# Layernorm statistics copied across the partitions by DMA instead of by TensorE, and other orders of work in front of the output projection

## What is computed

```
x = x + attention(layernorm(x), ctx, mask, Wq, Wk, Wv, Wo)   # 32 query heads, 8 key/value heads of 128, rope,
                                                             # logits = 30 * tanh(logits * 0.0884 / 30), mask, softmax
x = x + ffn(layernorm(x), W_base, b_base, W_router, A, B)    # one linear layer with a top-2 of 8 low-rank experts
layernorm(x) = (x - mean(x)) / sqrt(var(x) + 1e-5)           # mean and variance of each token (row) over 1024 features
```

## Time and profile before

| | us |
|---|---|
| median of 3 executions | 2128.66 (2127.95 to 2129.84) |
| the profiled execution, its own time | 2128.13 |
| its span in the trace | 2126.3 |
| TensorE busy in the span | 2118.6 |
| VectorE busy | 1652.2 |
| ScalarE busy | 879.3 |
| GpSimd busy | 338.8 |
| DMA | 508.52 MB, mean 239 GB/s |

### The profile page before, as it was taken

How to read it: one execution, slowest core, us unless ns; L and a number is a source line. 1 busy time by engine, 2 the same in 40 slices (tenths; PEclk the granted TensorE clock), 3 DMA queues, 4 the chain that set the end, 5 groups by cost and what they waited for, 6 DMA issues and landing times.

```text
span 2126.3 us, 26531 instructions
## 1 busy us (share of the span) xinstructions
PE 2118.6 (100%) x9429; PEld 1721.3 (81%) x9429; DVE 1652.2 (78%) x2387; ACT 879.3 (41%) x1353; POOL 338.8 (16%) x438
## 2 busy tenths in 40 slices
PE   9999999999999999999999999999999999999999
PEld 8888888888888888877777877777787777888887
DVE  6969759999986666677877888998999898856533
ACT  3323343222241111157555556655666566423211
POOL 0000025666350000003111111111111110100000
PEclk9999999999999999999999999999999999999999
DMA  8778667777685566679656666678557854596761
GB/s 314 244 247 287 237 208 303 277 282 267 258 320 210 211 216 212 219 249 314 226 190 197 232 238 198 198 257 290 199 171 264 295 197 153 191 359 247 283 248 61
DMA packets 198820, 508.52 MB, mean 239 GB/s; under 512 B 20896, under 2 KB 46624, under 8 KB 196640
## 3 DMA queue, kind: packets, MB, share of 16 engines
q1 hardware_dynamic: 172448, 424.43, 56.6%
q0 software_dynamic: 26240, 82.38, 11.6%
HBM read 357.26 MB, written 149.16 MB: 238 GB/s over the span
## 4 chain that ended last, share of the span: by engine, by line
PE 97%; DMA 1%; ACT 1%; DVE 0%; issue 0%; SPq 0%; ACTq 0%; DVEq 0%
PE pq L235 32%; PE pq L236 31%; PE pq L237 31%; PE pq L1300 1%; PE pq L1959 0%; PE pq L1958 0%; DMA raw<-gran 0%; DMA raw<-ctxT 0%; DMA RB<-rD 0%; DMA rD<-r 0%; PE pq L411 0%; ACT Rh L1225 0%; SPq L1122 0%; DVE Rl L1230 0%; ACT Pf L1439 0%
## 5 line engine op out<-in xcount | busy, mean ns | idle before, releaser
L235 PE MATMUL pq<-Ah,Rh 128*128 128x512 f32 x1024 | 399.0, 390 | 0.0
L237 PE MATMUL pq<-Ah,Rl 128*128 128x512 f32 x1024 | 398.5, 389 | 0.0
L236 PE MATMUL pq<-Al,Rh 128*128 128x512 f32 x1024 | 398.5, 389 | 0.0
L235 PE MATMUL pq<-Xq,qW 128*128 128x512 f32 x896 | 348.7, 389 | 0.5 <-issue 0.4
L236 PE MATMUL pq<-Xq,qW 128*128 128x512 f32 x896 | 348.6, 389 | 0.0
L237 PE MATMUL pq<-Xq,qW 128*128 128x512 f32 x896 | 348.5, 389 | 0.0
L1230 DVE TENSOR_TENSOR Rl<-raw,Rh 128x1024 fp32r<-128x1024 f32 x176 | 214.2, 1218 | 91.4 <-ACT Rh L1225 91.0
L1225 ACT ACTIVATE Rh<-raw 128x1024 fp32r<-128x1024 f32 x176 | 185.3, 1054 | 166.2 <-PE pq L237 128.2
L235 PEld LDWEIGHTS pq<-Ah,Rh 128*128 128x128 f32 x1024 | 192.2, 188 | 41.9 <-ACT Y L1451 0.8
L237 PEld LDWEIGHTS pq<-Ah,Rl 128*128 128x128 f32 x1024 | 192.2, 188 | 40.5
L236 PEld LDWEIGHTS pq<-Al,Rh 128*128 128x128 f32 x1024 | 192.2, 188 | 40.1
(11 more groups left out here) (243 smaller groups left out, 3935.2 us busy)
## 6 DMA issues: line engine op xcount, KB each, us to landing
raw<-gran SPq DMA_DIRECT2D x177, 512.0 KB, 4.4
QSD<-qW SPq DMA_DIRECT2D x64, 512.0 KB, 2.9
qD<-qt SPq DMA_DIRECT2D x128, 256.0 KB, 5.4
qW<-QSD SPq DMA_DIRECT2D x64, 512.0 KB, 3.4
qf<-qD SPq DMA_DIRECT2D x64, 512.0 KB, 6.1
RB<-rD POOLq DMA_DIRECT2D x128, 256.0 KB, 4.2
qraw<-gran SPq DMA_DIRECT2D x48, 512.0 KB, 5.2
kD<-kst SPq DMA_DIRECT2D x32, 512.0 KB, 5.7
```

The costliest lines, as they stand in the source:

```text
L235: e.matmul(dst, lh, rh, start=first, stop=False, skip_group_check=more)
L236: e.matmul(dst, lh, rl, start=False, stop=False, skip_group_check=more)
L237: return e.matmul(dst, ll, rh, start=False, stop=last, skip_group_check=more)
```

## The change

The statistics are spread by DMA. A new function `rows_spread` on POOL's queue, once for each chunk, writes each of the two columns of `mv` (mean and reciprocal deviation) to `rD` in DRAM, element by element, and reads it back as a row on all partitions, straight into `xl0` or `xl1`. The mean comes without the minus sign, so the addition on DVE and POOL becomes a subtraction. The diagonals on DVE, their splits on ACT and DVE, the 16 matmuls with ones and the 8 copies from PSUM are gone.

In front of O: on ACT the high part of query block 5 stands ahead of granule 9, and granule 11 behind the tanh of score block 4; on DVE the low part of block 5 stands ahead of granule 9's, those of granules 10 and 11 come earlier, and value product 0 leaves PSUM after product 1 and behind the low part of P. On POOL the stores of values 0 and 1 stand behind the loads of `RB`. On SP the loads of granules 12, 13 and 14 are put at steps -7 to -5 and that of group 1's values at -5.

```diff
-        DIAG = {15: 0, 16: 1, 38: 2, 39: 3}
-        SPREAD = {18: (0, 0), 19: (0, 1), 20: (1, 0), 21: (1, 1), 41: (2, 0), 42: (2, 1), 43: (3, 0), 44: (3, 1)}
...
-                if n in SPREAD:
-                    c, i = SPREAD[n]
-                    whole, high, low = diagonal(c, i)
-                    t.wait_ge("kv_dgl", (c, i))
...
-                    e.matmul(ps[7][:, :], ones[:, :], high[:, :], start=True, stop=False)
-                    e.matmul(ps[7][:, :], ones[:, :], low[:, :], start=False, stop=True).then_inc(*t.tick("kv_sp", (c, i)))
...
-                        t.wait_ge("kv_x", (i, 0))
-                        e.tensor_tensor(y, y, m[:, :], ALU.add).then_inc(*t.tick("kv_xa", (0, k, i, kk // 4)))
+                        t.wait_ge(f"d_xl{i}0", i)
+                        e.tensor_tensor(y, y, m[:, :], ALU.subtract).then_inc(*t.tick("kv_xa", (0, k, i, kk // 4)))
...
+        def rows_spread(t, c):
+
+            e = t.e
+            t.wait_ge("kv_rs", (c, 5))
+            for i in range(2):
+                e.dma_start(rD[i, c, :].rearrange("(b p) -> p b", p=P), mv[:, c, :, i], allow_slow_non_contiguous=True).then_inc(
+                    *t.tick(f"d_mv{i}", c, 16))
+            if c > 1:
+                t.wait_ge("kv_xn", (0, 3, c % 2))
+            for i in range(2):
+                t.wait_ge(f"d_mv{i}", c)
+                e.dma_start((xl1 if c % 2 else xl0)[i][:, :], bc(rD[i, c:c + 1, :], [P, T])).then_inc(*t.tick(f"d_xl{c % 2}{i}", c, 16))
+
         def pool_kv(t):
             e = t.e
+            rows_spread(t, 0)
+            rows_spread(t, 1)
             for k, i in XBLOCK.values():
...
+            rows_spread(t, 2)
+            rows_spread(t, 3)
...
-            if at == -10:
-                w_high(t, 11)
             if at == -9:
                 v_high(t, at)
...
+            if at == -10:
+                w_high(t, 11)
...
                 if at == -11:
+                    q_high2(t, 5)
                     w_high(t, 9)
-                    q_high2(t, 5)
...
-        V_EVAC = {-9: (0, 1), -8: (2,), -7: (3,), -6: (4,), -4: (5,), -2: (6,), 0: (7,)}
+        V_EVAC = {-9: (1, 0), -8: (2,), -7: (3,), -6: (4,), -4: (5,), -2: (6,), 0: (7,)}
...
+            if at == -9:
+                w_low(t, 11)
             for gi, b in S_AT.get(at - 1, []):
...
             if at == -9:
-                w_low(t, 11)
                 row_sums(t, 0)
-                v_low(t, at)
+                v_low(t, at, (1,))
...
             if at == -11:
                 q_low2(t, 4)
+                q_low2(t, 5)
                 w_low(t, 9)
-                q_low2(t, 5)
...
+            if at == -9:
+                v_low(t, at, (0,))
...
-            v_store(t, at)
+            if at == -8:
+                v_store(t, -9)
+            if at != -9:
+                v_store(t, at)
...
-            if at == -9:
+            if at == -5:
                 load_v(t, 1)
...
-            WL_AT.setdefault(at + 1, []).append(x)
+            WL_AT.setdefault({12: -7, 13: -6, 14: -5}.get(x, at + 1), []).append(x)
```

More of the change, by code:

```diff
@@ L40 @@
     "low": ("kv_lo", "q_lo", "w_lo"), "high": ("kv_hi", "q_hi", "w_hi"), "rope": ("kv_rope", "q_rope"),
-    "prep": ("kv_dg", "kv_dgl", "kv_bn", "kv_rs", "kv_mask", "kv_xb", "set", "q_xl0", "q_xl2"), "kv_low": ("kv_kl", "kv_vl", "v_vl"),
-    "kv_high": ("kv_kh", "kv_vh", "v_vh"), "prep_act": ("kv_sq", "kv_dgh", "kv_x"), "p": ("a_exp", "a_ph"),
+    "prep": ("kv_bn", "kv_rs", "kv_mask", "kv_xb", "set", "q_xl0", "q_xl2"), "kv_low": ("kv_kl", "kv_vl", "v_vl"),
+    "kv_high": ("kv_kh", "kv_vh", "v_vh"), "prep_act": ("kv_sq",), "p": ("a_exp", "a_ph"),
     "top": ("f_lg", "f_m8", "f_ix", "f_pr", "f_ixf", "f_oh", "f_w", "f_wx", "f_r2"), "f_act": ("f_e", "f_h", "f_hwh"),
@@ L58 @@
 SHARED_DMA += [(f"d_rb{i}", [f"d_bx{i}"]) for i in range(4)]
+SHARED_DMA += [(f"d_{x}{i}", [f"d_{y}{i}"]) for x, y in (("rt", "mv"), ("rs", "xl0"), ("x2", "xl1")) for i in range(2)]
 SHARED_DMA += [(f"d_x1{k}", [f"d_xt{k}"]) for k in range(4)]
@@ L462, in act_kv @@
             for n in range(-1, NK + 3):
[L463 to L469, removed]
                 for p in range(NPC):
@@ L487, in act_kv @@
                         e.activation(rs4[:, 1 + c % 2], rs4[:, 0] if c % 2 == 0 else rs4[:, 3], ACT.Sqrt).then_inc(*t.tick("kv_sq", c))
[L488 to L493, removed]
                 if 0 <= n - 1 < NK and KJ[n - 1][0] == "V":
@@ L572, in dve_kv @@
                         e.tensor_tensor(va, t1, t2, ALU.mult).then_inc(*t.tick("kv_rs", (c, 5)))
[L573 to L589, removed]
                 if n == MASK - 2:
@@ L763, in q_sum @@
             if n == 0:
-                t.wait_ge("kv_sp", (3, 1))
+                for i in (1, 3, 4, 5):
+                    t.wait_ge(f"d_xs1{i}", (0, 3))
             elif n < 15:
@@ L814, in x_block @@
                     t.wait_ge(f"d_bx{b}", k)
-                    t.wait_ge("kv_x", (3, 1))
-                    e.tensor_tensor(y, y, m[:, :], ALU.add).then_inc(*t.tick("q_xa", (k, b)))
+                    t.wait_ge(f"d_xl{b // 2}0", 2 + b // 2)
+                    e.tensor_tensor(y, y, m[:, :], ALU.subtract).then_inc(*t.tick("q_xa", (k, b)))
                 if what == "mult":
                     t.wait_ge("q_xa", (k, b))
+                    t.wait_ge(f"d_xl{b // 2}1", 2 + b // 2)
                     e.tensor_tensor(y, y, s[:, :], ALU.mult).then_inc(*t.tick("q_xm", (k, b)))
@@ L1475, in v_high, with v_low @@
                 e.activation(v_place(n)[:, 0, :], ps[v_bank(n)][:, :], ACT.Copy).then_inc(*t.tick("v_vh", n))
-        def v_low(t, at):
+        def v_low(t, at, which=range(8)):
             e = t.e
-            for n in V_EVAC.get(at, []):
+            for n in [x for x in V_EVAC.get(at, []) if x in which]:
                 t.wait_ge("v_vh", n)
@@ L1536, in dve_step @@
                 e.tensor_tensor(Y[:, m, :], ps[ring_bank(n)][:, :], Y[:, m, :], ALU.add).then_inc(*t.tick("y_add", n))
-            for x in [y for y in SPLIT.get(at, []) if at < 0 and y not in (5, 7, 8, 9, 10, 11, 12)]:
+            for x in [y for y in SPLIT.get(at, []) if at < 0 and y not in (5, 7, 8, 9, 11, 12)]:
                 w_low(t, x)
@@ L1558, in dve_step @@
                 q_low2(t, 4)
+                q_low2(t, 5)
                 w_low(t, 9)
-                q_low2(t, 5)
-            for x in [y for y in SPLIT.get(at, []) if at >= 0 and at != 4 or y in (8, 10)]:
+            for x in [y for y in SPLIT.get(at, []) if at >= 0 and at != 4 or y == 8]:
                 w_low(t, x)
```

15 lines of the change are left out of this document (2 added, 13 removed).

## The result

The changed kernel takes 2147.19 us (median of 6 runs, 2144.25 to 2152.96) against 2128.81 for the kernel before beside it: a ratio of 1.0087, 95% interval 1.0071 to 1.0104. Slower by 18 us, where the prediction had 7 us faster. The profiled execution took 2150.66 us by its own time, with a span of 2148.8.

What follows compares the result with a forecast made beforehand. TensorE's queue was taken as the bound; 3.68 + 1.50 + 1.54 = 6.72 us off the profiled 2128.13 gave 2121.41, and 2121.9 as the median, which lies 0.53 above that execution; range 2120.5 to 2125.2.

Steps and rivals of the forecast that it cites:

- Statistics, removed: Statistics on TensorE: 16 matmuls with ones fewer at 0.23 us each, 3.68 us off its queue.
- Statistics, added: POOL's queue: 16 DMAs, 5 us a write and 4.2 a read, 19 of 44 us available, so cost 0.
- TensorE waits for none now: Added DMA traffic could hold up a weight granule by about 4.2 us, but TensorE waits for no granule: cost 0.
- The rival of slow single numbers: POOL's writes of 512 single numbers spread badly, chunk 1's second read too late: 96 us slower, 2218; chance 0.04.
- t = 18: In the rival of slow single numbers, the time in us for a write beyond which VectorE is late.
- Hole A: In front of O, TensorE's wait for query block 5's low part, 1.19 plus 0.11 us, goes whole.
- the small stop: In front of O, TensorE's wait for granule 11's low part, 958.38 to 958.81, 0.20 us, goes.
- Hole B: In front of O, TensorE's 1.54 us loss from 975.88 to 977.65 goes, with RB 3.8 us earlier, 3.0 needed.
- I see no new wait: After both holes go, O's first product is late next, following TensorE's own pace; no new wait.

Runs made afterwards that it cites:

- e_64apart: Kernel before with only statistics by DMA, single numbers written 64 B apart, reads taken from the input: 2125.08 us against 2128.67.
- e_runs32: Kernel before with only statistics by DMA, one write per chunk of 128 runs of 32 B, read back in wrong order: 2124.71 us against 2128.67.
- e_apart: Kernel before with only statistics by DMA, single numbers written 512 B apart, reads taken from the input: 2124.54 us against 2128.80.
- e_front: Kernel before with only the changed orders and loads in front of O, statistics still by products with ones: 2127.53 us against 2128.80.
- e_turn_front: Kernel before with statistics turned by TensorE and written in runs of 512 B, plus the changed orders in front of O: 2124.98 us against 2129.06.
- e_late_loads: Kernel before with the changed orders in front of O, stores of values 0 and 1 behind values 2 to 5, SP's loads unmoved: 2127.35 us against 2128.71.
- e_stats: Kernel before with only the statistics by DMA, orders in front of O as before: 2151.58 us against 2128.80.
- e_close: Kernel before with only statistics by DMA, single numbers written side by side, reads taken from the input: 2144.19 us against 2128.67.

## Why the prediction was wrong

*Statistics, removed: 3.68 us.* Right, as far as these runs can tell. With writes that disturb nothing, the kernels without the 16 matmuls are faster than the kernel before by 3.6 (`e_64apart`), 4.0 (`e_runs32`) and 4.3 us (`e_apart`), and each of these differences is uncertain by about 2 us.

*Statistics, added: cost 0.* **This is the step that failed**, in two places. First the size: a write was taken as 5 us, from the row of `rD<-r` with its runs of 64 B, and measured 14.2 to 20.5. That row was near in bytes and partitions and far in what the runs show to count, how close together the small writes land: its numbers go out as runs of 64 B and not singly. Second, and worse, the mechanism: the sum asked only when the write lands, found 18 us harmless, and costed the traffic of the writes by their bytes (2 KB each). The time was lost elsewhere. VectorE's first use of the spread rows, at 141.96, did not wait for them: chunk 0's reads had landed by 110.5, and chunk 1's, the last issued at 124.42 and landed at 128.2, are first used at 152.35. It was the key stores, natural rows and granules of SP's queue that took 10 to 23 us beside the writes, where they took 4 to 8 before. "TensorE waits for none now" was read from a trace in which the engines moved 204 to 276 GB/s there; it said nothing of 55 to 187.

*The rival of slow single numbers* had the right sign and the chance of 0.04. Its mechanism, VectorE late for its own rows from t = 18 on, was wrong: a write of 16 us was below its threshold, the rows were there in time, and 21 us were lost all the same (24.7 less 3.7 saved). What the Trainium skill was cited for beside it pointed the right way and deserved more weight than that, since no row before showed single numbers at all and the bounds reached from 3.7 to 77 us.

*Hole A and the small stop, 1.50 us.* Right: gone in the changed kernel and in `e_front`.

*Hole B, 1.54 us.* The way was right and its condition was not met. In `e_front` RB came early enough and hole B went, as worked out. The step "I see no new wait" failed: the stores of values 0 and 1 behind RB's reads were counted as a relief for RB only, not as eight stores ahead of the one whose staging buffer ScalarE needs next. Of 3.04 us of gain 1.3 was left by the medians, 1.6 by the traces. With these stores later the front gives 3.2 us by the medians and 3.4 by the traces, the size of the sum. In the changed kernel itself hole B kept 1.0 us: the reciprocals' write took 6.72 us there, where I had taken 4.5, and 5.71 in `e_front`. Why it took longer there is not settled; `e_turn_front`, with no single numbers, shows it too (hole B 1.2).

*Together:* 24.7 lost in three stops, 3.7 saved and the front even makes 21.0 of the 22.5 us between the two profiled executions (2150.66 less 2128.13). Another 0.9 is a stop at 650, 1.9 us now and 1.0 in two parts before. It does not follow the change: it is as long in `e_late_loads`, which has the statistics as before, and 0.7 in `e_stats`. The rest is small.

## What to carry to other kernels

Before a DMA that writes single numbers to DRAM, look at how close together they land, and cost it by the transfers beside it, not by its bytes or its own landing: here the core moved a quarter to three quarters of the bytes while such writes ran. Turn the data on chip first so that the runs are long; two transposes cost 0.2 us here, and the stall was gone. And when stores are moved out of the way of one urgent transfer, find the buffer that each of them frees, and who needs it next.

## What the runs showed of the hardware that I had not expected

- 512 writes of 4 B side by side took 17.0 us (median of 8), the same 512 at 16 B distance 8.2, at 64 B 6.8, at 512 B 6.5. While they ran side by side in the changed kernel, the core's DMA rate over 8 us was 55 to 187 GB/s, where it was 204 to 276 before, at a DMA share of 0.63 to 1.18. Whether the place where they collide is the memory or the engines was not tried, nor whether it matters that neighbours came from different partitions.
- The size of the stall varies with what it meets: kernels with the same eight writes lost 19.9 (`e_stats`, and the change) and 12.0 us (`e_close`) in waits for granules from 90 us on, and their medians lie between 2144 and 2152 us. That `e_stats` is 4 us above the changed kernel, more than the front's 1.3, and 7 above `e_close` is left open.
- An operation of VectorE on 128x512 fp32 with one source read at a stride of 16 B took 1066 ns, with all contiguous 683.
